# Second attention in 16 two-head phases with one repeating period, and one image's convolution on GpSimd

## What is computed

```python
# layer 1
k = kernel * mask                      # 3x3, one filter per channel, centre weight 0
out = conv(x, k, 'SAME', feature_group_count=ch)
x = out + x
# layer 2
xp = jnp.pad(x, ((0, 0), (3, 3), (3, 3), (0, 0)), mode='reflect')
q = _to_heads(_conv1x1(x, Wq, bq), 8)
k = _to_heads(_conv1x1(xp, Wk, bk), 8)
v = _to_heads(_conv1x1(xp, Wv, bv), 8)
energy = jnp.einsum('bhdq,bhdk->bhqk', q, k)
attn = jax.nn.softmax(energy, axis=-1)
out = jnp.einsum('bhdk,bhqk->bhdq', v, attn)
return gamma * out + x
```

## Time and profile before

| | us |
|---|---|
| time before, median of 3 runs | 636.14 |
| lowest and highest of them | 633.23, 637.06 |
| the profiled execution's own time | 632.34 |
| its span, first to last instruction | 630.4 |
| PE busy | 542.9 (86%) |
| DVE busy | 389.1 (62%) |
| ACT busy | 355.0 (56%) |
| POOL busy | 75.0 (12%) |

### The profile page before, as it was taken

One profiled execution on the slowest core, in us unless ns is written; L12 is line 12 of the kernel. 1 busy time (PEld: TensorE's weight loads), 2 busy tenths in 40 slices (PEclk: granted clock), 3 DMA queues, 4 the chain that ended last, 5 costly groups with the idle time before them and its releaser, 6 DMA issues.

```text
span 630.4 us, 9426 instructions
## 1 busy us (share of the span) xinstructions
PE 542.9 (86%) x3600; PEld 286.9 (46%) x3600; DVE 389.1 (62%) x706; ACT 355.0 (56%) x678; POOL 75.0 (12%) x67
## 2 busy tenths in 40 slices
PE   6889988898996898889898898988998997677997
PEld 2665655554442333224333333322464483553886
DVE  2455644366388547475977977810555655866986
ACT  3677777775250423666576676748865625305553
POOL 5000000031047900203000000000520000000000
PEclk9999999999997587999999999959999998769999
DMA  8600000000000500053200000001300000000000
GB/s 306 264 3 1 2 2 2 1 2 1 0 1 1 91 11 1 0 91 65 47 1 1 1 1 1 1 2 46 131 1 2 1 1 0 2 0 0 1 33 34
DMA packets 5517, 18.10 MB, mean 29 GB/s; under 512 B 1632, under 2 KB 1760, under 8 KB 5088
## 3 DMA queue, kind: packets, MB, share of 16 engines
q1 hardware_dynamic: 5472, 17.50, 9.6%
HBM read 11.72 MB, written 1.05 MB: 20 GB/s over the span
## 4 chain that ended last, share of the span: by engine, by line
PE 68%; DVE 16%; ACT 13%; issue 2%; DMA 1%; SPq 0%; ACTq 0%; DVEq 0%
PE ps L435 60%; DVE mx L1357 9%; PE ps L587 5%; ACT r_p L1245 3%; ACT r_p L1103 2%; ACT r_p L1095 2%; PE ps L775 1%; ACT r_p L1067 1%; ACT r_p L1069 1%; DVE r_p L1580 1%; DVE r_prt L1574 1%; DVE r_p L1392 1%; DVE r_prt L1584 1%; DVE r_o L1397 1%; ACT r_stk L1085 1%
## 5 line engine op out<-in xcount | busy, mean ns | idle before, releaser
L1245 ACT ACTIVATE r_p<-ps 128x512 f32<-128x512 f32 x256 | 135.2, 617 | 83.7 <-PE ps L435 83.3
L1357 DVE TENSOR_REDUCE mx<-ps 128x2 f32<-128x1024 f32 x128 | 150.5, 1218 | 50.8 <-PE ps L435 50.6
L435 PE MATMUL ps<-stkr 48*128 48x512 f32 (+1 forms) x384 | 96.1, 482 | 17.3 <-DVE mx L1357 11.7
L435 PE MATMUL ps<-r_p,r_v 128*32 128x512 f32 (+3 forms) x832 | 86.0, 508 | 2.1 <-ACT r_p L1245 2.1
L435 PEld LDWEIGHTS ps<-stkr 48*128 48x128 f32 (+1 forms) x384 | 43.2, 198 | 96.3 <-DVE mx L1357 36.8
L1445 DVE CUSTOM_DVE_ANT_0 r_p<-ps,r_tab 128x209 f32<-128x209 f32 (+1 forms) x128 | 44.9, 401 | 32.0 <-PE ps L435 32.0
L1095 ACT ACTIVATE r_p<-r_p,mx 128x209 f32<-128x209 f32 (+1 forms) x128 | 57.8, 483 | 3.0 <-DVE mx L1445 2.9
L1103 ACT ACTIVATE r_p<-ps 95x512 f32<-95x512 f32 (+2 forms) x48 | 28.5, 593 | 33.7 <-PE ps L587 33.7
L587 PE MATMUL ps<-cst,r_p 128*95 128x128 f32 (+2 forms) x320 | 44.8, 280 | 1.8 <-ACT r_p L1095 1.1
L587 PEld LDWEIGHTS ps<-cst,r_p 128*95 128x95 f32 (+2 forms) x320 | 36.3, 150 | 18.5 <-ACT r_p L1095 9.2
L1453 DVE COPY r_p<-ps 95x512 f32<-95x512 f32 (+1 forms) x32 | 22.0, 686 | 24.4 <-PE ps L587 24.4
(11 more groups left out here) (199 smaller groups left out, 799.2 us busy)
## 6 DMA issues: line engine op xcount, KB each, us to landing
r_tab<-in_tab SPq DMA_DIRECT2D x4, 836.0 KB, 13.9
r_tab<-in_w SPq DMA_DIRECT2D x1, 2688.0 KB, 10.4
stkr<-nhi SPq DMA_DIRECT2D x32, 64.0 KB, 2.3
cst<-in_cst SPq DMA_DIRECT2D x1, 1124.5 KB, 18.5
r_tab<-in_tab SPq DMA_DIRECT2D x2, 532.0 KB, 7.4
r_tab<-in_tab SPq DMA_DIRECT2D x1, 1064.0 KB, 10.1
xt<-in_xT SPq DMA_DIRECT2D x4, 256.0 KB, 7.3
stkr<-nlo SPq DMA_DIRECT2D x16, 64.0 KB, 2.3
```

The costliest lines, as they stand in the source:

```text
L435: return nc.tensor.matmul(out, lhsT, rhs, start=start, stop=stop, **kw)
L1245: nc.scalar.activation(pa2[:, u % 12, :], ps[:, l2_bank(u), :], ACT.Exp).then_inc(sem("exp2"), 1)
L1357: v.tensor_reduce(mx[:, o:o + 2], ps[:, bank:bank + 2, :], AXIS.X, ALU.max).then_inc(sem("p1"), 1)
```

## The change

The convolution of the second image leaves TensorE and VectorE: GpSimd normalises that image, writes it to `pad` and does all nine taps, the centre as a copy and each of the others as one multiplication by a column and one addition over 1024 columns. The semaphore `x2b` says that it is done. For the first image TensorE now has three taps and VectorE six.

The attention now goes in 16 phases of two heads and 512 queries. One period r of the first pass is one "first" step; in the same period TensorE does two `l2_second` and one `l2_values`, twelve periods (`AHEAD`) behind. Within a period the order is a second product in rows 0 to 63, a first product in rows 64 to 127, a first product in rows 0 to 63, a second product in rows 64 to 127, and then the values of two periods ago: two heads times two halves of 256 queries. The jobs stand by period in `L2_JOBS`; three of block 0's steps (`values` of image 1 and two of the four `project2`) move into it, the others are re-timed. A turn has four transposes. The results of a phase stand in another layout, so the projection of the heads (`heads2`) is eight products of 64 rows and 256 columns for each tile.

```diff
-PE_TAPS = (1, 3, 4, 5, 7)
-DVE_TAPS = (0, 2, 6, 8)
+PE_TAPS = (1, 4, 7)
+DVE_TAPS = (0, 2, 3, 5, 6, 8)
...
+PH = 4 * NB
+PERIODS = 8 * PH
+AHEAD = 12
+L2_JOBS = {0: (("den", 4, 1), ("den", 5, 1)), 1: (("den", 6, 1), ("den", 7, 1)), 2: (("values", 0, 2),), 3: (("proj", 2, 1),), 5: (("proj", 3, 1),),
+           7: (("nproj", 1, 2),), 8: (("heads", 0, 2),), 10: (("gated", 0, 1),), 15: (("centre", 0, 2),), 16: (("centred", 0, 1),),
+           19: (("variance", 0, 2),), 44: (("nproj", 2, 2),), 47: (("values", 1, 2),), 60: (("nproj", 3, 2),)}
...
+            def l2_values(j):
+                m, c = j // 8, j % 8
+                b, pr, qh = phase(m)
...
+                pe.wait_ge(sem("exp2"), 2 * j + 2)
+                for half in range(2):
+                    for e in range(2):
+                        o = 64 * half + 32 * e
+                        last = mm(ps[o:o + 32, 7, 0:256], value2(b // NG * NCH + c, HG * (b % NG) + 2 * pr + e),
+                                  pa2[:, (2 * j + e) % 12, 256 * half:256 * half + 256], start=c == 0, stop=c == NCH - 1)
...
+            for q in range(PERIODS + AHEAD + 2):
+                p = q - AHEAD
+                if 0 <= p < PERIODS:
+                    l2_second(2 * p)
+                if q < PERIODS:
+                    first = ends[q - 1] if q else 0
+                    l2_entry(first)
+                if 0 <= p < PERIODS:
+                    l2_second(2 * p + 1)
+                if p >= 2:
+                    l2_values(p - 2)
+                if q < PERIODS:
+                    for e in range(first + 1, ends[q]):
+                        l2_entry(e)
...
+                elif kind == "nproj":
+                    if i == 1:
+                        pe.wait_ge(sem("sp2"), 3)
+                    elif i == 2:
+                        pe.wait_ge(sem("x2b"), 1)
...
+            def taps():
+                dst = x2[:, TOK:T].rearrange("p (r c) -> p r c", c=W)
+                src = [pad[:, 1, i // 3:i // 3 + H, i % 3:i % 3 + W] for i in range(9)]
+                pool.wait_ge(sem("rs"), 4)
+                pool.wait_ge(sem("pad0"), 1)
+                g.tensor_tensor(t1b, t1b, sq1, ALU.mult).then_inc(sem("ng"), 2)
+                pool.wait_ge(sem("ng"), 4)
+                g.tensor_scalar(pad[:, 1, 1:1 + H, 1:1 + W], t1b.rearrange("p (r c) -> p r c", c=W), vv("lng0"), vv("lnb0"),
+                                ALU.mult, ALU.add).then_inc(sem("lnout"), 2)
+                pool.wait_ge(sem("lnout"), 4)
+                g.tensor_copy(dst, src[4]).then_inc(sem("tap1"), 1)
+                done = 1
+                for j, i in enumerate((0, 1, 2, 3, 5, 6, 7, 8)):
+                    w = tapped[:, TOK * (j % 2):TOK * (j % 2 + 1)].rearrange("p (r c) -> p r c", c=W)
+                    if j > 1:
+                        pool.wait_ge(sem("tap1"), 2 * j - 1)
+                    g.tensor_scalar(w, src[i], vv(f"kc{i}"), None, ALU.mult).then_inc(sem("tap1"), 1)
+                    pool.wait_ge(sem("tap1"), 2 * j + 2)
+                    g.tensor_tensor(dst, dst, w, ALU.add).then_inc(sem("x2b" if j == 7 else "tap1"), 1)
```

More of the change, by code:

```diff
@@ L185 @@
-LOOSE = ("den", "heads", "gated", "centre", "centred", "norm")
-def l2_order():
-    order = []
-    for n in range(2 * NB):
-        for r in range(16):
-            order.append(("first", n, r))
-            if n and r == 1:
-                order.append(("max", n - 1, 0))
-            if (n, r) in L2_JOBS:
-                kind, i, parts = L2_JOBS[n, r]
-                if n == 0:
-                    order.append((kind, i, parts - 1))
-                else:
-                    order += [(kind, i, k) for k in range(parts)]
-    order.append(("max", 2 * NB - 1, 0))
+PH = 4 * NB
@@ L203, in l2_order, with phase @@
+def phase(m):
+    return m // 4, m // 2 % 2, m % 2
+def l2_order():
+    order, ends = [], []
+    for r in range(PERIODS):
+        order.append(("first", r, 0))
+        if r % 8 == 1 and r > 8:
+            order.append(("max", r // 8 - 1, 0))
+        for kind, i, parts in L2_JOBS.get(r, ()):
+            order += [(kind, i, k) for k in range(parts)]
+        if r == PERIODS - 1:
+            order.append(("max", PH - 1, 0))
+        ends.append(len(order))
     slot, done, at, c, p = [], [], {}, -1, 0
@@ L204, in l2_order @@
     for kind, i, k in order:
-        loose = kind in LOOSE or (kind, i) == ("nproj", 1)
-        c += kind in ("first", "max") or not (loose or k)
+        loose = (kind, i) in LOOSE
+        c += not (loose or k)
         p += kind in ("first", "max")
@@ L210, in l2_order @@
         at[kind, i, k] = len(slot) - 1
-    before = []
-    for n in range(2 * NB):
-        a = at["max", n, 0] + 1
-        b = at["max", n + 1, 0] + 1 if n + 1 < 2 * NB else a
-        before += [a + min((k + 1) * (b - a) // 28, b - a) for k in range(32)]
-    return order, slot, done, at, before
+    return order, slot, done, at, ends
 W3 = [("wq3", C), ("wk3", C), ("wv3", C), ("wo3", C), ("lkg", C), ("lkb", C), ("aw1", 2048), ("aw2", 512),
@@ L865, in _ @@
             for t in range(NT):
[L866 removed]
+                heads2(t)
             norm(1, lambda t: xt[:, tile(t)], "x3_ready")
@@ L1683, in _, with blank @@
             g.memset(zmax, 0.0).then_inc(sem("zero_max"), 1)
+            blanks = [0]
+            def blank(b):
+                for a in range(2):
+                    for rows in (slice(32, 64), slice(96, 128)):
+                        pool.wait_ge(sem("blank"), blanks[0]) if blanks[0] else pool.wait_ge(sem("zero_max"), 1)
+                        g.memset(stack(b)[rows, a, :, :].bitcast(F32), float(a)).then_inc(sem("blank"), 1)
+                        blanks[0] += 1
+            blank(1)
+            blank(3)
+            pool.wait_ge(sem("blank"), blanks[0])
             pool.wait_ge(sem("in_cst"), 16)
```

384 lines of the change are left out of this document (175 added, 209 removed).

## The result

Four executions of the changed kernel have a median of 617.0 us (610.8 to 630.0), four of the kernel before beside them 636.6 us: ratio 0.961, 95% interval 0.952 to 0.971. A second set, run as the first experiment, gave 614.7 us, ratio 0.965 (0.960 to 0.970). The range of 588 to 636 us holds both, and both lie 2 to 4 us above the forecast of 613. Executions differ in how long TensorE ran at its lower clock: the medians are of all of them, the ratios leave out the longest (here 621.1 and 630.0 us), and as the profiled one is that of 621.1 us, I read the second set's profile (613.0 us) beside it where lengths matter.

The account below looks back on a forecast made before the run. Bound: hand-overs between three nearly full engines. Start +5, lead-in +6, next 32 periods +23, wait -22, 84 periods -2, tail +13 make 23 us gained; `heads2` costs 1: 613 us from 636.1, range 588 to 636.

Parts of the forecast that it names:

- Up to the first score product: End of layer 0 to layer 2's attention: first score product at 170.3 us, 5.1 us gained; memsets at most 1 us.
- Lead-in: Attention's first 12 periods instead of 16, before the first second-pass product: 25.7 us, ending at 196.0 us.
- The period: Settled attention: 11.2 us a phase, 1.40 us a period against 1.56, with TensorE and VectorE each at 10.5 a phase.
- Rival 1: Settled attention: the period stays at 1.56 us, hand-overs limiting as before; costs 13.4 us, 626 us; chance 0.13.
- The start of GpSimd's chain: GpSimd's convolution of the second image starts when its normalisation (`rs`) is there: 216 us (213 to 222).
- The length of the chain: GpSimd's convolution takes 56 us, multiplications at 3.6 us and additions at 2.36, so `x2b` comes at 272 us.
- TensorE alone would be at period 44 at 250 us. It waits for `x2b` there, some 22 us: Projection needing the convolved second image: TensorE arrives at 250 us, including 5 for waits and clock, and idles until 272.
- Rival 2: GpSimd multiplies as fast as it copies: chain 34 us, `x2b` at 250, no wait; 586 us; chance 0.12.
- After `x2b`: To the attention's end at 417 us: 117.6 for 84 periods, 7 for jobs and stalls, 15 tail, 5 lower clock.
- The rest: Program behind the attention: `heads2` waits for four instead of two normalised tiles, +1 us.
- The forecast's last step: From 610 us by the profiled execution's measure to 613 us, as that execution lay 3.8 us under the median.
- Rival 3: TensorE's clock stays down after the wait for `x2b`: about 650 us for half the remaining time, 690 for all; chance 0.09.

Follow-up runs that it names:

- the first experiment: The changed kernel measured again with no edit: median 614.7 us, ratio 0.965 (0.960 to 0.970) to the kernel before.
- neither edit alone: Against the changed kernel (0.965): two-operation multiplications with later ones and zeros 608.5 us, 0.953; one small step for three 610.1 us, 0.957; all together 588.9 us, 0.925.

## Why the prediction was right, and what in it was not

The time came out within 4 us, but by luck: two errors, of 22 and 28 us, took each other away.

*Up to the first score product*: 15.4 us from the first `conv` product (160.38 to 175.78), forecast 15.0, 20.2 before. It came at 175.8 and not at 170.3, since layer 0, unchanged, ran 5 us later in this execution. The memsets beside the taps, priced at 1 us at most, cost 1.4 us on the first tap alone; with them elsewhere this stretch took 15.0 us, with them 15.4 and 16.5 in two profiles. Counted from the write of `pad` ahead of the tap, which was held too, it is 15.7 us without the memsets and 17.2 and 18.1 with them. So they cost 1.5 to 2.4 us here where the range had 1, and the kernel without them is 4 us faster by its ratio; where the rest is, if it is real, stays open.

*Lead-in*: the first `Exp` at 201.95 is 26.2 us behind the first score product, forecast 25.7.

*The period*: 11.17 us a phase in all settled ones, forecast 11.2, and for the reason given: halving what VectorE reads leaves 10.5, the sum made for TensorE; taking two of its small steps away leaves 10.76. Rival 1 is gone.

*The start of GpSimd's chain*, "216 us (213 to 222)": it was 229.5, of which 5 are the late layer 0. The step behind it, 20 us from the first second-pass product to `rs`, took 27.6: I had put 3 us of waits and lower clock, and the clock was at half for 20 us of that stretch.

*The length of the chain*, 56 us: 47.4. The term mis-sized is "a multiplication at 3.6 us" by the line through two rows: 2.85 at 1024 columns, and 1.20 for the one with two columns. Additions were 2.37 as read.

*"TensorE alone would be at period 44 at 250 us. It waits for `x2b` there, some 22 us"*: this is the step that failed. TensorE came at 275 to 278, with the chain, and waited 0.5 us at most. It was 5.5 us late at the first score product and lost the rest on the way, for the most part at half clock, where it was for 54.6 us between the first `Exp` and period 44 in this profile. The sum had 5 us for that; I had read the clock in the settled part (1.00), and did not ask what a GpSimd that is busy for 47 us on end does to VectorE's small steps, though rows of them stood there (0.17 us each). Not all of it is the taps': with the centre tap only TensorE still took 85.0 us from the first score product, where the sum has 79.7. The wait itself was right as a mechanism: it is there with the halved maxima, 9.6 us, and with a single small step, 14.9 us, and half clock for 13.7 us comes with that one. I had 14, but all of it on work and at a price of 5 us; 3.4 of the 13.7 us fell on work. Rival 2's chain of 34 us was made too, by the two-operation multiplications (33.6 us), and gave 8 us where the rival had 27, since TensorE was late for it.

The Trainium skill, page "GPSIMD Engine Reference", section "Specifications", says that GpSimd shares its SBUF interfaces with VectorE, with contention for VectorE instructions in a two-port mode or with two SBUF inputs. The rows agree for the small steps with both inputs in SBUF beside a GpSimd copy or multiplication (0.17 against 1.05 us), and for the maxima read from PSUM, which took 1.22 us beside GpSimd and without it. Beside memsets they don't: there the small steps with two SBUF inputs took 0.17 us and the taps 1.31 us each, as without them. The step with one SBUF input was held too; whether it ran in a two-port mode no run here shows.

*After `x2b`*: to the end of the attention 148.4 us (276.96 to 425.35), forecast 144.6; without the forecast fall of the clock behind a wait, but with one in the tail, which took 22.7 us for 15; at full clock it takes 15.2. *The rest* of the program grew by 3.5 us (425.35 to 619.3 against 439.9 to 630.4), where I had 1 for `heads2`. (The forecast's last step, 610 and 3.8 us, makes 614, not 613.)

Rival 3, the clock stays down, is the one that came in part: not behind a wait for `x2b`, but in its place, 20 to 34 us.

## What to carry to other kernels

Before moving elementwise work to an idle GpSimd, look at what VectorE does beside it, small steps on a chain above all: eight numbers took 1.05 us for 0.17, and in six of seven profiles with a turn that came 1.8 us late or more TensorE's clock fell. The fewer such steps stand in a row, the fewer can be held, and here it mattered whether the GpSimd instruction beside them read or only wrote. Two limits of nearly the same length hide each other; a chain that ends just as it is needed doesn't show that the chain is the limit, and neither edit alone told its worth (8 and 5 us, together 26). A sum that comes out right is no proof of its steps: here the wait forecast at 22 us was none, and it took kernels with less of the other cost to find 10 and 15 of it.

## What the runs showed of the hardware that was not expected

- GpSimd's `tensor_scalar` over 128x1024 takes 2.85 us with one operation on a column and 1.12 to 1.20 us with two.
- A GpSimd instruction on SBUF can hold a VectorE instruction that begins beside it: steps of 0.17 us took 0.5 to 2.3 us. The held step ended 0.02 to 0.04 us behind the GpSimd instruction, or 1.13 to 1.16 us behind the start of one of 2.85 us with a single operation.
- Beside a memset only VectorE instructions with one SBUF input were held (a step 0.93 us for 0.17, a tap 2.25 for 0.81); those with two were not (22 steps, and the taps of 1.31 us).
- TensorE was at half clock for 34.1 us, busy all the time, 2.5 us behind an idle time of 1.8 us; in the second set's profile the stretch behind the same turn was 20.5 us long.
